# Rows of two weight tables at a pitch of 1184 words instead of 1160, and column parts of 512, 320 and 328 instead of 512, 324 and 324

## The reference

```python
# layer 0: one adapter of 64 for each sequence, rank 16
Bx  = einsum('bni,bri->bnr', x, B0[adapter_ids])
x   = x + einsum('bnr,bor->bno', Bx, A0[adapter_ids])

# layer 1: a dense layer and 8 experts of rank 16, the best two of them per row
base    = einsum('btd,od->bto', x, W)
logits  = einsum('btd,ed->bte', x, Wr) + 5.0 * one_hot(language_ids, 8)
topw, topi = top_k(logits, 2)
gates   = sum(one_hot(topi, 8) * softmax(topw)[..., None], axis=-2)
h       = einsum('btd,erd->bter', x, A)
x = x + base + 2.0 * einsum('bter,bte,eor->bto', h, gates, B)
```

## Time and profile before

| | |
|---|---|
| Median of 3 runs | 544.13 us (544.03 to 545.87) |
| Profiled execution, span from the first to the last instruction | 544.8 us (no other time of it is on record) |
| TensorE matmul busy | 529.6 us, 97% of the span |
| TensorE weight load busy | 479.9 us, 88% |
| VectorE / ScalarE / GpSimd busy | 329.5 / 213.9 / 174.6 us |
| DMA | 60.42 MB, 111 GB/s on the mean |

### The profile page before, as it was taken

The page is one execution under the profiler, slowest core; times in us unless marked ns, Lnnn a source line. Parts: engine busy times, 40 slices in busy tenths (PEclk is TensorE's granted clock), DMA queues, the critical chain, the costliest instruction groups (busy, mean ns, idle before and its releaser), DMA issues.

```text
span 544.8 us, 9381 instructions
## 1 busy us (share of the span) xinstructions
PE 529.6 (97%) x3500; PEld 479.9 (88%) x3500; DVE 329.5 (60%) x829; ACT 213.9 (39%) x493; POOL 174.6 (32%) x162
## 2 busy tenths in 40 slices
PE   6897999999999999999999999999999999999997
PEld 5786998888999888899988889998888999888897
DVE  3888465666566566655656655565665557566421
ACT  4645234443333444333344433334443333444211
POOL 6462033332223333222333322233332223331100
PEclk9999799999999999999999999999999999999999
DMA  8933244422434442243444223344422434421101
GB/s 334 305 98 93 73 126 125 127 79 90 123 89 127 125 126 85 86 121 91 123 125 127 83 89 119 92 122 126 126 84 88 120 95 119 126 87 40 40 39 40
DMA packets 30865, 60.42 MB, mean 111 GB/s; under 512 B 4316, under 2 KB 20060, under 8 KB 30820
## 3 DMA queue, kind: packets, MB, share of 16 engines
q1 hardware_dynamic: 24144, 38.81, 23.3%
q0 software_dynamic: 6656, 20.98, 12.7%
q10 hardware_dynamic: 20, 0.03, 0.0%
HBM read 43.02 MB, written 16.78 MB: 110 GB/s over the span
## 4 chain that ended last, share of the span: by engine, by line
PE 90%; DVE 6%; DMA 2%; issue 1%; ACT 0%; another core or an unknown queue 0%; ACTq 0%; DVEq 0%
PE o_bank L453 73%; PE o_bank L467 8%; PE x_bank L372 5%; PE b_bank L354 3%; DVE w_lo L687 1%; DMA b_in<-in_L_cond_B_dram,b_run 1%; DVE a_raw L730 1%; DVE x_bank L712 1%; PE b_bank L342 1%; DMA ids<-in_itok_B_dram 0%; DVE x_lo L687 0%; DVE top_no L792 0%; PE b_bank L362 0%; DVE lb_t L702 0%; DVE b_raw L723 0%
## 5 line engine op out<-in xcount | busy, mean ns | idle before, releaser
L453 PE MATMUL o_bank<-w_hi,x_hi 128*128 128x512 f32 (+1 forms) x744 | 260.5, 350 | 0.0
L453 PE MATMUL o_bank<-w_hi,x_lo 128*128 128x512 f32 (+1 forms) x744 | 253.4, 341 | 0.0
L453 PE MATMUL o_bank<-w_lo,x_hi 128*128 128x512 f32 (+1 forms) x744 | 252.9, 340 | 0.0
L283 POOL TENSOR_TENSOR a_t<-a_raw,a_t 64x1024 fp32r<-64x1024 f32 x30 | 72.2, 2408 | 292.8 <-ACT a_t L575 292.8
L453 PEld LDWEIGHTS o_bank<-w_hi,x_hi 128*128 128x128 f32 x744 | 140.9, 189 | 15.8 <-issue 5.7
L453 PEld LDWEIGHTS o_bank<-w_hi,x_lo 128*128 128x128 f32 x744 | 140.6, 189 | 10.9
L453 PEld LDWEIGHTS o_bank<-w_lo,x_hi 128*128 128x128 f32 x744 | 141.0, 190 | 9.9
L626 ACT COPY out_sb<-o_bank 128x324 f32<-128x324 f32 (+1 forms) x96 | 40.0, 446 | 221.1 <-PE o_bank L467 221.1
L712 DVE STREAM_TRANSPOSE x_bank<-x_in 128x512 f32<-128x512 f32 x60 | 69.3, 1204 | 0.2
L258 POOL DMA_INDIRECT a_in<-in_L_cond_A_dram,a_run x64 | 62.6, 978 | 19.2 <-issue 19.2
L730 DVE STREAM_TRANSPOSE a_raw<-a_in 128x1024 f32<-128x1024 f32 x32 | 65.2, 2038 | 0.0
(11 more groups left out here) (102 smaller groups left out, 438.0 us busy)
## 6 DMA issues: line engine op xcount, KB each, us to landing
out_dram<-out_sb SPq DMA_DIRECT2D x31, 512.0 KB, 2.6
x_in<-in_x_dram SPq DMA_DIRECT2D x120, 128.0 KB
w_in<-in_L_cond_W_dram SPq DMA_DIRECT2D x6, 512.0 KB, 12.5
x_in<-in_x_dram SPq DMA_DIRECT2D x2, 512.0 KB
out_sb<-in_L_cond_W_dram SPq DMA_DIRECT2D x2, 512.0 KB, 14.3
a_in<-in_L_cond_A_dram,a_run POOLq DMA_INDIRECT x64
w_in<-in_L_cond_A_dram SPq DMA_DIRECT2D x1, 512.0 KB, 4.4
b_in<-in_L_cond_B_dram,b_run POOLq DMA_INDIRECT x32
```

The source lines that it names most:

```text
L283: nc.gpsimd.tensor_tensor(lower, a_raw[Q:P, :], lower.bitcast(F32), ALU.subtract).then_inc(a_lo_ready, 1)
L453: mm = pe.matmul(O[part][:, 0:hi - lo], xs[:, n % 2, c, :], w[:, c, lo:hi], start=(k == 0), stop=(k == K3 - 1), skip_group_check=True)
```

## The change

`LINE` is 32 words, 128 bytes. The pitch of a row of `w_hi` and `w_lo` goes from NW = 1160 words (4640 bytes) to `PITCH` = 1184 words (4736 bytes, 37 x 128); the last 24 words of a row are neither written nor read. `REST` goes from 324 to 320, so `PARTS` becomes (0, 512), (512, 832), (832, 1160): 512, 320 and 328 columns. Part 2 starts at byte 3328 of a row instead of 3344. The slices of the B tables, the copies to `out_sb` and the stores of the last tile take their bounds from `PARTS` and follow. The number and the order of instructions stay as they were on each engine; two lines are added ahead of all of them, so a line number of before is 2 higher after.

```diff
--- before.py
+++ after.py
@@ -31,14 +31,16 @@
     ER = E * R
     NH = ER + E
     NW = NH + D
-    REST = (NW - BANK) // 2
+    LINE = 32
+    PITCH = (NW + LINE - 1) // LINE * LINE
+    REST = (NW - BANK) // 2 // LINE * LINE
     PARTS = [(0, BANK), (BANK, BANK + REST), (BANK + REST, NW)]
     NP = len(PARTS)
     K3 = 3 * C
     Q = P // 2
     NWB = D // P
     G = P // SQ
-    assert ER == P and BR == SQ and HB == 2 and REST % 2 == 0 and F == SQ * C and D == SQ * SQ
+    assert ER == P and BR == SQ and HB == 2 and F == SQ * C and D == SQ * SQ
 
 
     x_rows = x.rearrange("b s d -> (b s) d")
@@ -61,8 +63,8 @@
         def sem(name):
             return ctx.enter_context(nc.semaphore(name))
 
-        w_hi = sb("w_hi", [P, C, NW], F32R)
-        w_lo = sb("w_lo", [P, C, NW], F32R)
+        w_hi = sb("w_hi", [P, C, PITCH], F32R)
+        w_lo = sb("w_lo", [P, C, PITCH], F32R)
         lb_hi = sb("lb_hi", [P, D], F32R)
         lb_lo = sb("lb_lo", [P, D], F32R)
         ident = sb("ident", [P, P])
```

## The result

The changed kernel takes 546.7 us (median of 20 runs, 544.85 to 547.7), the kernel before 544.99 us (20 runs, 544.03 to 546.04). The ratio is 1.0029 with a 95% interval of 1.002 to 1.0037. So it is slower by 0.3%, a real difference, though smaller than the 0.5% that I had called the limit of a measurement here. The prediction, 544.1 us and no effect, was wrong: the time lies 0.3 us outside the range of 542.0 to 546.4 us. Of the 2.6 us between forecast and result, 0.9 us is the starting point (the median of before was 544.13 us over 3 runs and 544.99 us over 20), and 1.7 us is the effect. Neither alone would have left the range.

The account below looks back on a forecast made before the run. The prediction took the start-to-start spacing of TensorE's matmuls as the bound. Its terms summed to 0 against the 544.8 us span; with the 544.13 us median it forecast 544.1 us, range 542.0 to 546.4 us.

Parts of the forecast that it names:

- That the matmuls of the loop set the time, nothing waits, and only the spacing of matmuls matters: Main loop: PE busy for all of a 15.88 us tile, 31 tiles making 492 us; everything else has slack.
- The widths, price 0: Parts 1 and 2: 320 + 328 columns stream the same 648 as 324 + 324; 43 ns shorter and as much longer.
- The alignment: 0 in the forecast: Table rows starting at 0 modulo 128 bytes: price 0, bounded by 1.6 us gained and 3.6 us lost.
- My upper bound: Part 0: all eight rows take 0.71 us instead of a mean of 0.696; 0.12 us a tile, 3.6 us in all.
- c = 4 of part 0: An already aligned table row of the kernel before: 0.71 us for its three matmuls, neighbouring rows 0.69 to 0.70 us.
- show nothing on either side: Parts 1 and 2: aligned row 0.45 us against 0.443 and 0.447; 148.2 against 148.6 ns a matmul; reason for price 0.
- a poorer pace: Loop matmuls: a new layout costs some 1.5 ns on each of 81 a tile; 3.8 us slower, 547.9 us; chance 0.09.
- lines of 128 bytes: Parts 0 and 1: fewer lines touched at about 1.2 ns each; 1.6 us saved, 542.5 us; chance 0.07.
- widths in steps: Parts 1 and 2: width charged in steps of 8 columns; 3.0 us saved, 541.1 us; chance 0.08 with other gains.
- The rule of 16-byte lines: Table accesses: penalty only on crossing 16-byte lines early; all rows were aligned already, so the sum would be 0.
- The sign of being wrong that I gave: Main loop: a forecast of no change is wrong if the tile is shorter or longer by more than 88 ns.
- part 0 moving from 232 ns: Part 0, changed in addresses alone: if its time a matmul moves, alignment matters, on the side to which it moves.

Follow-up runs that it names:

- e2_widths: Changed kernel with rows back at the old pitch of 1160 words, parts 512, 320 and 328 columns; ratio 0.9991 to the kernel before, tile 15.886 us.
- e10_x64_324: Changed kernel with x1 at 64 instead of 96 modulo 128 bytes and the old widths of 324 and 324 columns; tile 15.852 us.
- e1_pitch: Changed kernel with the old widths of 324 and 324 columns, so the pitch alone is changed; 547.93 us, ratio 1.0032 to the kernel before.
- e8_before_x64: Kernel before with x1 at 64 instead of 96 modulo 128 bytes; tile 15.953 us.
- e16_1216_d128: Changed kernel at a pitch of 1216 words, x1 moved by padding so every table row starts 128 modulo 256 bytes from x1; tile 15.914 us.
- e4_x64: Changed kernel with x1 at 64 instead of 96 modulo 128 bytes; tile 15.808 us; timed as the same kernel again, 545.13 us, ratio 0.9966 to the kernel before.
- e3_rows32: Changed kernel with the two tables 32 bytes further on; 543.85 us, ratio 0.9955 to the kernel before.
- e5_x0: Changed kernel with x1 at 0 instead of 96 modulo 128 bytes; tile 15.840 us.
- e15_1216_d0: Changed kernel at a pitch of 1216 words, x1 moved by padding so every table row starts 0 modulo 256 bytes from x1; tile 15.813 us.

## Why the prediction was wrong

- **That the matmuls of the loop set the time, nothing waits, and only the spacing of matmuls matters: right.** PE is busy for all of the changed kernel's tile, and its loop is 2.1 us longer without a wait.
- **The widths, price 0: right.** e2_widths: 0.9991, and +6 ns a tile. It isn't a general 0: with x1 moved the same exchange of columns makes 44 ns (e10_x64_324).
- **"The alignment: 0 in the forecast": the step that failed.** The pitch alone costs 66 ns a tile, 2.0 us in all, and a ratio of 1.0032 (e1_pitch). My upper bound, 0.12 us a tile for all rows like c = 4 of part 0, had the right place and sign (all rows of part 0 become like c = 4), and the measured +60 ns of part 0 is half of it; 0.71 us of a printed row was 0.704 us unrounded. I then took the value from parts 1 and 2, which "show nothing on either side". They were the wrong neighbours: the narrow matmuls feel the place less (+2 ns at most, in part 2 of e8_before_x64 and of e16_1216_d128), and part 0 is where the 512-column ones are. The nearest row was the aligned row of the same width, and it was the slowest of its part (234.6 ns).
- **The reading of "aligned" was wrong as well.** I asked where a row starts modulo 128. Where it starts against x1, which was at 96, counts too: moving x1 alone took the whole loss back and more (e4_x64). The four offsets in the trace were four distances. The change took away the mixture, and left the one distance that turned out the poorest of the five tried at its pitch.
- **The rival "a poorer pace": right in kind, at 0.09.** Its sentence "or make every row like c = 4 of part 0" is what happened; its size, 3.8 us, was about twice too large. Its reason against itself, that the aligned c = 4 of part 1 is ordinary, is the step above once more.
- **The other rivals fell:** lines of 128 bytes (it would have gained), widths in steps.
- **The rule of 16-byte lines in the Trainium skill ("SBUF — State Buffer", "SBUF: two separate sides")** gave the same 0 as I took. Shifts by 32 bytes modulo 128, which keep every row on a multiple of 16 bytes, move a tile by up to 0.14 us here, so that rule doesn't bound what a layout can do.
- **The range and the baseline:** I took the median of three runs as it stood, 544.13 us, though the profiled span, 544.8 us, lay above it. In the runs after it the time lies 1.8 us over the span (546.85 against 545.0 us). The sign of being wrong that I gave, a tile more than 88 ns longer, was too coarse: 69 ns came. The other one, part 0 moving from 232 ns, was the right one: 234.3.

**What stays open.** Shown is that the pitch costs the time, that moving either the tables or the stationary operand changes the pace at full clock with the same instructions, and that the matmuls fall into repeating cycles of one to six. That it is the distance between the two, and not their two places, rests on one pair of kernels (e3_rows32 and e4_x64), and distance alone is not the whole of it (e8_before_x64; and e5_x0, with distances of 0 and 128 modulo 256 by turns, had 231.6 ns, where the two alone average 230.7). What in the memory or in TensorE makes the cycle, whether places modulo more than 256 bytes matter, and a formula for the pace I don't have.

## What to carry to other kernels

Where TensorE is the bound with no waits and streams wide float32r rows, try two or three placements of the stationary operand and the tables relative to each other (32-byte steps of padding): it takes 128 to 256 bytes of each partition, and here it moved the time by 0.75% between the slowest and the fastest layout timed on one chip (e1_pitch 547.93, e3_rows32 543.85 us). Rounding a pitch up to a "clean" number makes all rows alike, which helps or harms by where they meet the other operand. And before resizing a part of a loop, look at what hides behind it: 1.4 us less of part 0 met 0.5 us of slack and cost 31 us.

## What the runs showed of the hardware

- At full clock (2.4 GHz) a matmul with a new stationary operand costs about (columns + 32) / 2.4 GHz from start to start, where it runs most evenly: in e15_1216_d0 the 320-column ones settle at 146.7 ns, the 328-column ones at 150, and the 512-column ones at 226.7 = 544 / 2.4 ns. Other layouts lie up to 2 ns above this at 320 to 328 columns and 2 to 8 ns above it in the mean of part 0. At half clock there is no such addition: 324 columns took 270 ns and 320 columns 266.7 ns, whatever the place.
- The kernel before repeats its tiles within 1 ns (15.879 to 15.881 us) from 102 us on, over 400 us, in spite of DMA and three other engines at work. The changed kernel's alternate between 15.946 and 15.953 us, and one of them, two thirds through the loop, is 15.920. This is why one profile tells layouts apart (66 ns a tile, 2 us in all) that timed runs, which scatter over 5 us (543.26 to 548.48 us for the kernel before on one chip), barely tell.
- The length of a tile may differ by 140 ns between layouts that differ in nothing but the place of x by 32 bytes modulo 128 (changed kernel and e4_x64).
